# The first FFN of a graph network kernel: gates ahead of the expert matmul, Green recursion begun behind them, adjacency moved behind it

## The reference

```
v = jnp.clip(x @ v_w + v_b, -V_MAX, V_MAX)                 # V_MAX = 3
a = (-2.0 + v).astype(jnp.complex64) - 1j
G = bk_green_diag(a)                                       # d_i = a_i - 1/d_(i-1), e likewise from the end,
feats = jnp.stack([G.real, G.imag], axis=-1)               # G = 1/(d + e - a), over the 128 rows
logits = x @ gate_w + gate_b
topv, topi = jax.lax.top_k(jax.nn.softmax(logits), 2)      # two of 8 experts
comb = sum of one_hot(topi) * topv / sum(topv)
h = gelu(einsum('bnd,edf->bnef', x, w1) + b1)              # 8 experts of 48 columns
ffn_out = einsum('bne,bned->bnd', comb, einsum('bnef,efd->bned', h, w2) + b2)
return ffn_out + bk_scale * (jnp.clip(feats, -10, 10) @ out_w + out_b)
```

## Time and profile before

| | |
|---|---|
| median of 3 runs | 357.82 us (357.77 to 357.97) |
| profiled execution, its own time | 358.23 us |
| its span, first to last instruction | 356.4 us |
| granted TensorE clock, mean | 1.000 of full speed (2.4 GHz) |
| busy of the span: TensorE, VectorE, ScalarE, GpSimd | 97%, 51%, 19%, 11% |
| shares of the chain that ended last: TensorE, VectorE, DMA, ScalarE | 82%, 10%, 4%, 1% |

### The profile page before, as it was taken

The page is one execution under the profiler, slowest core; times in us unless marked ns, Lnnn a source line. Parts: engine busy times, 40 slices in busy tenths (PEclk is TensorE's granted clock), DMA queues, the critical chain, the costliest instruction groups (busy, mean ns, idle before and its releaser), DMA issues.

```text
span 356.4 us, 4226 instructions
## 1 busy us (share of the span) xinstructions
PE 345.9 (97%) x1606; PEld 216.5 (61%) x1606; DVE 180.4 (51%) x545; ACT 67.6 (19%) x157; POOL 38.4 (11%) x62
## 2 busy tenths in 40 slices
PE   7999999999999999989999999999999999999997
PEld 3566656665665656546455655575546598966754
DVE  3946336585838384567752644432851501163431
ACT  2002111011110101002110331022313422074120
POOL 4900000020000000141022000040122100000000
DMA  7999999998973849999996567574761610000001
GB/s 268 421 368 432 430 413 424 425 417 318 350 268 114 375 163 390 419 359 407 402 426 216 217 257 262 203 283 178 265 236 57 244 67 3 0 2 0 0 2 44
DMA packets 10502, 90.19 MB, mean 253 GB/s; under 512 B 2169, under 2 KB 2822, under 8 KB 6386
## 3 DMA queue, kind: packets, MB, share of 16 engines
q1 hardware_dynamic: 8238, 84.91, 60.2%
q0 software_dynamic: 848, 3.61, 2.8%
q10 hardware_dynamic: 1396, 1.40, 1.2%
HBM read 89.53 MB, written 0.39 MB: 252 GB/s over the span
## 4 chain that ended last, share of the span: by engine, by line
PE 82%; DVE 10%; DMA 4%; issue 1%; ACT 1%; SPq 1%; POOL 0%; DVEq 0%
PE ps L1467 13%; PE ps L1501 13%; PE ps L1446 7%; PE ps L1873 7%; PE ps L1693 5%; PE ps L1674 4%; DMA ring<-in_gat_w 4%; PE ps L1489 3%; PE ps L1785 2%; PE ps L1567 2%; PE ps L1985 2%; PE ps L1944 2%; PE ps L2005 2%; PE ps L1378 2%; DVE ring L877 2%
## 5 line engine op out<-in xcount | busy, mean ns | idle before, releaser
L1467 PE MATMUL ps<-ring,xT 128*128 128x512 f32 (+1 forms) x168 | 56.7, 486 | 0.4 <-DMA ring<-in_gat_w 0.4
L1501 PE MATMUL ps<-ring,h 128*128 128x512 f32 (+1 forms) x168 | 55.6, 486 | 0.0
L1501 PEld LDWEIGHTS ps<-ring,h 128*128 128x128 f32 x168 | 31.2, 190 | 21.9 <-issue 20.1
L1467 PEld LDWEIGHTS ps<-ring,xT 128*128 128x128 f32 x168 | 30.9, 191 | 19.9 <-issue 16.9
L496 ACT ACTIVATE h<-ps 128x768 f32<-128x768 f32 (+6 forms) x24 | 13.8, 577 | 60.8 <-PE ps L1467 16.2
L789 DVE CUSTOM_DVE_ANT_0 g<-h,avec 128x768 f32<-128x768 f32 x8 | 7.7, 959 | 35.0 <-ACT h L496 22.3
L1446 PE MATMUL ps<-ring,xT 128*128 128x512 f32 (+1 forms) x72 | 24.1, 488 | 0.1
L877 DVE TENSOR_SCALAR ring<-ring,idxb,ewb 128x128 bf16<-128x128 bf16 x99 | 24.1, 325 | 0.0
L1378 PE MATMUL ps<-shiftm 128*128 128x512 bf16 x64 | 19.3, 427 | 2.8 <-POOL shiftm L388 2.1
L382 POOL TENSOR_TENSOR rstd<-var,mhalf 128x1 f32<-128x1 f32 x8 | 4.7, 582 | 140.5 <-DVE var L731 69.0
L1446 PEld LDWEIGHTS ps<-ring,xT 128*128 128x128 f32 x72 | 13.4, 190 | 9.3 <-issue 8.4
(11 more groups left out here) (400 smaller groups left out, 496.2 us busy)
## 6 DMA issues: line engine op xcount, KB each, us to landing
ring<-in_gat_w SPq DMA_DIRECT2D x15, 2304.0 KB, 11.4
avec<-in_gat_a SPq DMA_DIRECT2D x9, 768.0 KB, 10.4
ring<-in_l_w SPq DMA_DIRECT2D x3, 2304.0 KB, 16.1
ring<-in_gat_w SPq DMA_DIRECT2D x6, 384.0 KB, 6.2
ring<-in_l_w SPq DMA_DIRECT2D x2, 1152.0 KB, 12.9
ring<-in_l1f_w1a SPq DMA_DIRECT2D x1, 2304.0 KB, 13.2
ring<-in_l1f_w1b SPq DMA_DIRECT2D x1, 2304.0 KB, 10.5
ring<-in_l1f_w2a SPq DMA_DIRECT2D x1, 2304.0 KB, 12.2
```

Source lines behind the costliest of these rows:

```text
L1467: last = mm(ps[:, at + lo:at + hi], xT[:, c, :], w[:, c, lo:hi], start=(c == 0), stop=(c == C - 1))
L1501: last = mm(ps[:, 4 * WIN + lo:4 * WIN + hi], h2[:, par * D + c * P:par * D + (c + 1) * P], w[:, c, lo:hi], start=(n == 0 and c == 0), sto ...
```

## The change

The gate matmuls run by themselves; all six expert chunks stand behind them, spread between the shifts of levels 0 to 2 (one ahead of shift 0, two ahead of shift 1, two ahead of shift 2, one behind it). The 2 is subtracted in the bias row ahead of time, and clip and copy to the four places of the state are one instruction. The choice of two is a maximum of eight and a match with replacement: whatever was replaced is chosen. `green_level` takes the small work as `meanwhile`, behind the masked state and ahead of the wait for the shift. Twelve warm matmuls behind shifts 1 to 3 become four behind shift 3; shift 4 stands ahead of the transposes of the weighted inputs, shift 5 behind them, and shift 6 behind both halves of the second layer's first chunk, which goes to banks 1 and 2.

The adjacency's sums and degrees stand behind the copy of `combT`, its half scaling behind the third part of the transposed rows, its transpose behind `product(3)` and its whole scaling ahead of the next gates; GpSimd's root of the degrees stands behind two loads that it used to precede. Semaphores of the two FFNs' hidden steps are joined into one counter each (`hid0_mm` and `hid1_mm` to `hid_mm`, and so on), and the wait for `adj_ready` moves to the first reader of `adj2T`.

The core of the diff:

```diff
             pool.memset(comb[:, 10:11], 1.0).then_inc(s("bk_const"), 1)
+            pool.memset(lin[:, E0 + 1:E0 + 7], -BIG).then_inc(s("bk_const"), 1)
             pool.memset(combT[:], 0.0).then_inc(s("bk_const"), 1)
             inverse_root(2)
-            inverse_degree_root(1)
             load_row(avec[:], "l1_b1", 2 * D)
             pool.wait_ge(s("tail_ready"), 1)
             pool.dma_start(g1[0:G1N * E1N, :], a["l1_b2"]).then_inc(s("in_b2"), 16)
-
+            inverse_degree_root(1)
...
             link(nc.vector.tensor_scalar(missing, missing, -1.0, 1.0, ALU.mult, ALU.add))
+            level_row = row("l0_gate")[:, E0:E0 + 1]
+            dve.wait_ge(S["small_in"], SMALL)
+            link(nc.vector.tensor_scalar(level_row, level_row, -2.0, None, ALU.add))
...
             part_T(2)
-            dve.wait_ge(s("edges_summed"), 1)
-            link(nc.vector.tensor_tensor(adj2T[:], bank(3, P, P), ident, ALU.add))
-            link(nc.vector.tensor_tensor(adj2T[:], adj2T[:], bank(3, P, 2 * P), ALU.add))
-            link(nc.vector.tensor_tensor(adj2T[:], adj2T[:], bank(3, P, 3 * P), ALU.add))
-            half_adjacency(1, adj2T)
...
                     .then_inc(S["dve_step"], 1)
                 used["dve_step"] += 1
+                if meanwhile is not None:
+                    meanwhile()
                 dve.wait_ge(s("shifted"), lv + 1)
...
+            dve.wait_ge(s("bk_const"), 11)
             link(scaled(lin[:, 0:E0 + 1], bank(7, E0 + 1), row("l0_gate")))
-            link(nc.vector.tensor_scalar(level, lin[:, E0:E0 + 1], 3.0, -3.0, ALU.min, ALU.max))
-            link(nc.vector.tensor_scalar(level, level, -2.0, None, ALU.add))
-            dve.wait_ge(s("bk_const"), 10)
-            nc.vector.tensor_copy(directions[:, :, 0:6:5], level.unsqueeze(2).broadcast_to([P, 2, 2])) \
-                .then_inc(s("green_state"), 1)
-            dve.wait_ge(s("constants"), 6)
-            pick_first(1, lin[:, 0:E0], 1, E0)
-            green_level(0)
-            whole_adjacency(1, adj2T)
-            pick_second(lin[:, 0:E0], 1, E0)
-            green_level(1)
-            top_shares(1, comb[:, 0:E0], 1, E0)
-            green_level(2)
...
+            nc.vector.tensor_scalar(directions[:, :, 0:6:5], lin[:, E0:E0 + 1].unsqueeze(2).broadcast_to([P, 2, 2]), 1.0, -5.0,
+                                    ALU.min, ALU.max).then_inc(s("green_state"), 1)
+            def best_two():
+                link(nc.vector.max(best, lin[:, 0:E0]))
+                nc.vector.tensor_scalar(weight, lin[:, 0:E0], best[:, 0:1], None, ALU.subtract).then_inc(s("top_shifted"), 1)
+                nc.vector.tensor_scalar(level, lin[:, E0:E0 + 1], 1.0, -5.0, ALU.min, ALU.max).then_inc(S["dve_step"], 1)
+                used["dve_step"] += 1
+            def marked():
+                link(nc.vector.memset(best[:, 2:8], -BIG))
+                link(nc.vector.match_replace(left, best, lin[:, 0:E0 + 7], BIG))
+                link(nc.vector.tensor_tensor(chosen, left[:, 0:E0], lin[:, 0:E0], ALU.not_equal))
+            def shares():
+                dve.wait_ge(s("top_exped"), 1)
+                link(nc.vector.tensor_tensor_reduce(weight, weight, chosen, 1.0, 0.0, ALU.mult, ALU.add, weight_sum))
+                link(nc.vector.reciprocal(weight_sum, weight_sum))
+                link(nc.vector.tensor_scalar(comb[:, 0:E0], weight, weight_sum, None, ALU.mult))
+            def expert_inputs():
+                dve.wait_ge(s("hid_mm"), 1)
+                scaled(h1[:, 0:H0], bank(0, H0), row("l0_b1")).then_inc(s("hid_ready"), 1)
+            def expert_shares():
+                dve.wait_ge(s("gelued"), 1)
+                nc.vector.tensor_tensor(grouped(h1[:, 0:H0], E0, F0), grouped(h1[:, 0:H0], E0, F0),
+                                        wide(comb[:, 0:E0], E0, F0), ALU.mult).then_inc(s("hid_scaled"), 1)
+            green_level(0, best_two)
+            green_level(1, marked)
+            green_level(2, shares)
+            green_level(3, expert_inputs)
+            green_level(4, expert_shares)
+            green_level(5)
+            green_level(6)
...
             nc.vector.tensor_copy(combT[0:11, :], bank(7, P, 0, 11)).then_inc(s("combT_ready"), 1)
-            add_residual(2, 2 * WIN, x)
+            dve.wait_ge(s("edges_summed"), 1)
+            link(nc.vector.tensor_tensor(adj2T[:], bank(3, P, P), ident, ALU.add))
+            link(nc.vector.tensor_tensor(adj2T[:], adj2T[:], bank(3, P, 2 * P), ALU.add))
+            link(nc.vector.tensor_tensor(adj2T[:], adj2T[:], bank(3, P, 3 * P), ALU.add))
+            degrees(1, adj2T)
+            add_residual(2, WIN, x)
             normalise(3, xn, x, "xn_ready")
             part_T(3)
+            half_adjacency(1, adj2T)
...
             part_T(4)
+            whole_adjacency(1, adj2T)
...
                 last = mm(bank(7, E0 + 1), xT[:, c, :], gatew[:, c * (E0 + 1):(c + 1) * (E0 + 1)],
                           start=(c == 0), stop=(c == C - 1))
-                if c in (1, 3):
-                    hidden_first(c // 2)
             last.then_inc(s("gate_ps"), 1)
-            turn_adjacency(1, adj2T)
...
+            hidden_first(0)
+            shift_green(0)
+            hidden_first(1)
             hidden_first(2)
-            shift_green(0)
-            for c in range(3, C):
-                last = hidden_first(c)
-            last.then_inc(s("hid0_mm"), 1)
-            for lv, n in ((1, 4), (2, 4), (3, 4)):
-                shift_green(lv)
-                stay_warm(n, 1)
-            pe.wait_ge(s("hid0_scaled"), 1)
+            shift_green(1)
+            hidden_first(3)
+            hidden_first(4)
+            shift_green(2)
+            hidden_first(5).then_inc(s("hid_mm"), 1)
+            shift_green(3)
+            stay_warm(4, 1)
+            shift_green(4)
+            pe.wait_ge(s("hid_scaled"), 1)
             for c in range(3):
                 last = tr(ps[:, 4 * WIN + c * P:4 * WIN + (c + 1) * P], h1[:, c * P:(c + 1) * P], ident)
-            shift_green(4)
             stay_warm(2, 1)
+            shift_green(5)
...
             for c in range(3):
                 for lo, hi in HALVES:
-                    last = mm(ps[:, 2 * WIN + lo:2 * WIN + hi], h1[:, H0 + c * P:H0 + (c + 1) * P], w[:, c, lo:hi],
+                    last = mm(ps[:, WIN + lo:WIN + hi], h1[:, H0 + c * P:H0 + (c + 1) * P], w[:, c, lo:hi],
                               start=(c == 0), stop=False)
-                    if c == 0:
-                        shift_green(5 if lo == 0 else 6)
+                if c == 0:
+                    shift_green(6)
...
             product(3, U_L1, "l1_w", 0, "rows_ps")
+            turn_adjacency(1, adj2T)
             warm_until(5, "var_ready", 4)
```

More of the change, by code:

```diff
@@ L577, in _ @@
             nc.scalar.activation(tk[:, 3, 0:E0], tk[:, 3, 0:E0], ACT.Exp).then_inc(s("top_exped"), 1)
[L578 to L581, removed]
+            act.wait_ge(s("hid_ready"), 1)
+            nc.scalar.activation(h1[:, 0:H0], h1[:, 0:H0], ACT.Gelu_apprx_tanh).then_inc(s("gelued"), 1)
+            act.wait_ge(s("hid_ps"), 1)
+            copy(h1[:, H0:2 * H0], ps[:, 4 * WIN:4 * WIN + H0]).then_inc(s("hidT"), 1)
             act.wait_ge(s("l2_ps"), 1)
@@ L584, in _ @@
             act.wait_ge(s("l2_ps"), 2)
-            copy(up_first, bank(1, HID2, 0, DOWN + 1)).then_inc(s("l2_copied"), 1)
+            copy(up_first, bank(0, HID2, 0, DOWN + 1)).then_inc(s("l2_copied"), 1)
             part_T(3)
@@ L595, in hidden_gelu @@
             def hidden_gelu(g):
-                act.wait_ge(s("hid1_ready"), g + 1)
+                act.wait_ge(s("hid_ready"), g + 2)
                 nc.scalar.activation(h1[:, g * H0:(g + 1) * H0], h1[:, g * H0:(g + 1) * H0], ACT.Gelu) \
-                    .then_inc(s("gelu1"), 1)
+                    .then_inc(s("gelued"), 1)
             def hidden_T(g):
-                act.wait_ge(s("hid1_ps"), g + 1)
-                copy(h2[:, g * H0:(g + 1) * H0], bank(4 + g % 2, H0)).then_inc(s("hid1T"), 1)
+                act.wait_ge(s("hid_ps"), g + 2)
+                copy(h2[:, g * H0:(g + 1) * H0], bank(4 + g % 2, H0)).then_inc(s("hidT"), 1)
             hidden_gelu(0)
@@ L840, in _, with degrees @@
             deg, root = cell("degree", 2), cell("deg_root", 2)
+            def degrees(n, adjT):
+                nc.vector.tensor_reduce(deg[:, n:n + 1], adjT[:], AX.X, ALU.add).then_inc(s("degree"), 1)
             def half_adjacency(n, adjT):
-                nc.vector.tensor_reduce(deg[:, n:n + 1], adjT[:], AX.X, ALU.add).then_inc(s("degree"), 1)
                 dve.wait_ge(s("deg_root"), n + 1)
@@ L870, in _ @@
             link(nc.vector.tensor_tensor(adj1T[:], count[:], ident, ALU.add))
+            degrees(0, adj1T)
             half_adjacency(0, adj1T)
@@ L988, in _, with green_level @@
             directions = state.rearrange("p (d m) -> p d m", m=16)
-            def green_level(lv):
+            def green_level(lv, meanwhile=None):
```

(24 more changed lines are left out.)

32 lines of the change are left out of this document (17 added, 15 removed).

## The result

The changed kernel takes 355.96 us (median of four executions, 355.2 to 356.56) beside 357.89 for the kernel before: ratio 0.9936, interval 0.9925 to 0.9948. Timed once more, again beside the kernel before, it takes 355.14 (354.9 to 355.21) beside 358.32: ratio 0.9909, interval 0.9894 to 0.9925. The granted clock was 1.000 in all eight executions.

What follows compares the result with a forecast made beforehand. The prediction took a latency chain between TensorE and VectorE in the first FFN as the bound: 2.8 us gained through the levels less 0.05 for the adjacency, 2.75 off 357.82, gives 355.07, stated as 355.0, range 354.2 to 356.3.

Steps and rivals of the forecast that it cites:

- the walk: The first FFN's chain between TensorE and VectorE, priced step by step on the trace's clock: 2.75 us gained.
- Gates by themselves: First FFN's gate matmuls without expert chunks between them take 1.53 us, lin starts 1.25 us sooner (bounds 1.25 and 1.43).
- Setting the state: Ahead of level 0, lin and one step of 0.17: state ready at 162.80, total gain so far 1.62 us.
- Levels 0 to 2: VectorE ends last in level 0, TensorE in 1 and 2; states at 164.35, 165.95 and 167.76 us.
- rival A: New VectorE operations in levels 0 and 1 are slow, 0.96 each: gain 1.85 us, 356.0; chance 0.05.
- Rival B: Shifts behind queued chunks take 0.63 in levels 0 to 2 and 6: gain 1.6 us, 356.2; chance 0.04.
- Levels 3 and 4: Level 3 ends 2.35 us ahead; level 4, its shift no longer behind weighting and transposes, 3.0 ahead.
- Level 6: Its shift stands behind both halves of the first second-layer chunk: TensorE costs 0.3 us, level ends 2.7 ahead.
- Adjacency: Its sums and degrees between combT's copy and the residual are just covered by VectorE's idle time: 0.05 us lost.
- Rival C: Gain not kept, as the tail's load lands only when used now: 357.8 us, no change; chance 0.03.
- Rival D: Clock falls to 1.2 GHz, say in level 3, with fewer warm matmuls: 5.75 us more, 363.6; chance 0.04.

Runs made afterwards that it cites:

- e1: Changed kernel with the first two expert chunks back between the gate matmuls: 356.20 us, ratio 0.9940.
- e7: Kernel before with only its gate matmuls by themselves, the first two expert chunks behind them and the adjacency's transpose: 359.66 us, ratio 1.0042.
- e8: Changed kernel with level 4's shift back behind the weighting of the expert inputs and their three transposes: 356.73 us, ratio 0.9969.
- e3: Changed kernel with level 6's shift behind one half of the first second-layer chunk in place of both: 355.08 us, ratio 0.9908.
- e11: Changed kernel with the adjacency back in front, but its transpose behind the first expert chunk: 356.4 us, ratio 0.9962.
- e6: Changed kernel with the adjacency back in front, its transpose right behind the gate matmuls: 357.99 us, ratio 0.9990.
- e9: Changed kernel without the two warm matmuls behind the transposes, the four behind shift 3 kept: 356.06 us, ratio 0.9946.
- e2: Changed kernel without its six warm matmuls between the shifts: 357.32 us, ratio 0.9966.
- e4: Changed kernel with the old choice of two experts (six, seven and four small VectorE operations) in levels 0 to 2: 356.6 us, ratio 0.9957.

## Why the prediction was right

The mechanism is the predicted one: a chain between two engines, shortened at its links, with the gain kept to the end. That 2.75 stands so near the 2.88 of the trace is in part luck: the walk was 0.22 short, and 0.11 lost behind the next gates, which it did not have, took half of that back. By its own steps:

- **Gates by themselves.** lin 1.28 sooner for 1.25 taken (gates 1.48 for 1.53). Right; but e1 prices the step at 0.97 within the whole, since level 1 is 0.32 longer with both chunks behind the gates, and e7 at nothing alone. The walk had the longer level 1 (1.60 for 1.41) without setting it against this step.
- **Setting the state**: as walked (0.43 from lin's start for 0.44); what the edit is worth by itself was not run.
- **Levels 0 to 2.** In level 0 the forecast had VectorE end last, 0.21 behind the shift, by four steps of 0.20; they took 0.59 in all, from 163.71 to 164.30, and the shift ended last by 0.04. So sum 0 came 0.17 ahead of the walk. TensorE ended last in levels 1 and 2, as forecast, and as its queue set the time this was worth nothing: sums 1 and 2 lie within 0.04 of the walk. Maximum 0.16, match 0.09 and 0.16, memset 0.06 us, for the 0.20 each that I took: rival A is out. The match is two instructions, as the Trainium skill ("VectorE: DVE Perf Modes", section "Two Vector instructions with no wait between them") has it; the 0.2 estimated by it for level 1 did not appear, for the shift ended last there by 0.35.
- **Rival B** is out: the shifts behind chunks took 0.35 to 0.40.
- **Levels 3 and 4** hold the term that was mis-sized: 8.17 and 9.7 walked, 8.01 and 9.43 measured. I added rows end to end; the bias of the expert inputs began 0.10 ahead of the masked state's end, the products 0.05 ahead of the bias's, the weighting 0.11 ahead of level 4's masked state. By the copy of combT the walk is 0.27 long, where 0.1 was allowed; with the 0.05 of the adjacency that was not lost, this is the difference between 2.75 and 2.97. The order of level 4 is worth 0.98 (e8). Its shift took 0.62, the time of a shift by itself, for the 0.35 walked, and ended at 170.72, the weighting at 170.74: nothing was lost, but the 0.45 between the two in the walk was gone.
- **Level 6** lost 0.32 for the 0.3 walked (e3).
- **Adjacency.** Cost 0.00 behind combT for 0.05 taken: combT to residual is 1.53 in both kernels. In front it cost 0.6 (e11), and more with TensorE's stop and the clock (e6).
- **Rival C** is out: no load is waited for behind 177 us.
- **Rival D** did not occur in the eight executions, but stands nearer than its 0.04 sounds. The kernel before has it too, in one of the 68 executions timed beside the experiments (360.35, clock 0.995). My reason against it, that TensorE is at least as busy after the change, held (13.96 us of the 15 from 162 to 177, second profile, for 13.74); yet two warm matmuls fewer let the clock fall in four of six executions (e9). And the clock fell where I had not looked, in e7 and e6, at the expert chunks behind the gates. The price was too high: 8.5 lost (the 5.75 and the 2.75 gained), where e2 lost 2.2, since its clock was back at 1.00 by 177, ahead of product 3.
- **Not foreseen**: 0.1 lost behind the next gates, in every run built on the changed kernel, with the old choice (e4) and with the adjacency in front (e6, e11) too: 157.05 to 157.08 against 156.97, and 156.96 in e7. Half of it stands at the next lin; what causes it was not found.

The parts are not a sum: undone one at a time (e1, e4, e8, e11) they cost 1.0, 1.1, 1.0 and 0.6, which is more than the 2.97 together, and the gates alone (e7) gain nothing. Each link is worth its length only while the others are short enough to let it end last.

The predicted 355.0 lies 0.96 under the first measurement and 0.14 under the second; what lies between the two is told above and is not of the program.

## What to carry to other kernels

Walk a latency chain stage by stage with both engines' clocks and ask at every link which one ends last; put long independent work ahead of a short dependent step, which then takes 0.35 for 0.63, but only so much that it ends with the other engine's work: with two chunks ahead of its shift level 1 took 1.80 from sum to sum, with one (e1) 1.48. Before warm matmuls are removed, or a short stop is put ahead of a stretch of small matmuls, look at the granted clock in several executions, since one profile at 1.00 does not settle it. A part that is right in the whole can be worth nothing alone, so a step by itself is a poor trial of it.

## What the runs showed of the hardware

The clock did not fall in the same way each time: one and the same program had it at 1.00 in some executions and 0.995 over the span in others (e9 two and four, e6 five and seven, e7 three and nine, e8 eight and four, e11 seven and four, with one at 0.999). By the medians of each run the executions with the fall were 1.0 to 1.9 us longer. In the changed kernel all eight stood at 1.00, in the kernel before all but one of 68 at 0.999 or more.

The half scaling took 0.84 in place of 0.28, while GpSimd's add ran from 183.74 to 185.55 (first the row of the kernel before, then the add):

```profile
162.74 0.28 DVE L846 TENSOR_SCALAR adj2T<-adj2T,cells 128x128 f32<-128x128 f32 x1 [0.66 <-POOL cells L422]
...
183.74 1.81 POOL L414 TENSOR_TENSOR xb<-x,row 128x768 f32<-128x768 f32 x1 [1.05 <-DVE xn L738]
```

It was hidden in the wait for product 3. That the two engines share a way to the memory is the Trainium skill's ("GPSIMD Engine Reference", section "1. Specifications": contention with VectorE's instructions in a two-port mode or with two inputs in that memory). The rows fit it: the scaling takes 0.28 to 0.29 in the four profiles where it stands in front with no add beside it (the kernel before, e6, e7, e11). Whether the scaling runs in such a mode no run shows, and none moved the add by itself.
